# Cross-attention block on Trainium2: Q with its bias row kept in its PSUM bank instead of the SBUF staging tile

## What is computed

```python
g_x     = (g_w @ x_2 + g_b).transpose          # (N, CI)   CI = 256, C = 512, N = 1024
theta_x = (theta_w @ x + theta_b).transpose    # (N, CI)
phi_x   = phi_w @ x_2 + phi_b                  # (CI, N)
W  = theta_x @ phi_x / N
y  = (W @ g_x).transpose
wy = w_w @ y + w_b
wy = bn_gamma * (wy - bn_mean) * rsqrt(bn_var + 1e-5) + bn_beta
out = wy + x
```

## Time and profile before

| what | us |
|---|---|
| median of three runs | 796.55 |
| the profiled execution, its own time | 797.28 |
| its span, first to last instruction | 795.5 |
| PE busy | 778.5 (98%) |
| POOL busy | 540.8 (68%) |
| DVE busy | 524.7 (66%) |
| ACT busy | 305.4 (38%) |

### The profile page before, as it was taken

One profiled execution on the slowest core, in us unless ns is written; L12 is line 12 of the kernel. 1 busy time (PEld: TensorE's weight loads), 2 busy tenths in 40 slices (PEclk: granted clock), 3 DMA queues, 4 the chain that ended last, 5 costly groups with the idle time before them and its releaser, 6 DMA issues.

```text
span 795.5 us, 11592 instructions
## 1 busy us (share of the span) xinstructions
PE 778.5 (98%) x4045; PEld 665.4 (84%) x4045; DVE 524.7 (66%) x889; ACT 305.4 (38%) x514; POOL 540.8 (68%) x358
## 2 busy tenths in 40 slices
PE   4999999999999999999999999999999999999997
PEld 4688888888888888888888888888888888888886
DVE  3787584857758497584857758497584857758254
ACT  3734442325334143442325334143442325334131
POOL 4969785777857579585777857579585777857500
PEclk9999999999999999999999999999999999999999
DMA  9828255171643707255171633707255171630202
GB/s 235 195 107 211 107 117 201 33 219 67 167 150 73 243 0 211 105 115 201 31 220 65 167 149 73 243 0 211 105 117 200 29 223 64 168 150 1 106 1 105
DMA packets 55127, 103.17 MB, mean 130 GB/s; under 512 B 2474, under 2 KB 37956, under 8 KB 55108
## 3 DMA queue, kind: packets, MB, share of 16 engines
q1 hardware_dynamic: 52976, 101.86, 43.7%
q10 hardware_dynamic: 2132, 1.05, 0.8%
HBM read 69.35 MB, written 33.55 MB: 129 GB/s over the span
## 4 chain that ended last, share of the span: by engine, by line
PE 96%; DVE 2%; ACT 1%; DMA 1%; issue 0%; DVEq 0%; SPq 0%; ACTq 0%
PE wbank L667 56%; PE gbank L667 36%; PE wbank L830 1%; DMA ctx_sb<-in_ctx_dram 1%; PE wbank L708 1%; PE wbank L686 0%; ACT ctxT_hi L340 0%; DVE x_sb L486 0%; PE wbank L714 0%; ACT x_sb L366 0%; DVE ctxT L486 0%; DVE th_lo L583 0%; DVE tmp L509 0%; DVE tmp L508 0%; ACT x_hi L340 0%
## 5 line engine op out<-in xcount | busy, mean ns | idle before, releaser
L286 POOL TENSOR_TENSOR ctxT_lo<-ctxT,ctxT_hi 128x512 fp32r<-128x512 f32 x124 | 167.6, 1353 | 200.1 <-ACT ctxT_hi L340 200.1
L297 POOL TENSOR_TENSOR ctx_sum<-ctx_sum,ctxT 128x512 f32<-128x512 f32 x108 | 163.7, 1516 | 0.2
L315 POOL TENSOR_TENSOR x_lo<-x_sb,x_hi 128x1024 fp32r<-128x1024 f32 x60 | 142.4, 2406 | 0.0
L340 ACT ACTIVATE mt<-wbank 128x512 fp32r<-128x512 f32 x64 | 37.9, 597 | 242.7 <-PE wbank L667 242.7
L657 DVE SCALAR_TENSOR_TENSOR x_sb<-wbank,const,x_sb 128x512 f32<-128x512 f32 x112 | 79.2, 747 | 67.6 <-PE wbank L667 67.6
L667 PE MATMUL wbank<-ctxT_lo,ctxT_hi 128*128 128x512 f32 x512 | 121.0, 392 | 0.0
L518 DVE TENSOR_TENSOR stage<-gbank,mt 128x384 f32<-128x384 f32 x64 | 28.3, 485 | 139.8 <-PE gbank L667 139.7
L667 PEld LDWEIGHTS wbank<-ctxT_lo,ctxT_hi 128*128 128x128 f32 x512 | 95.1, 189 | 18.6 <-POOL ctxT_lo L286 0.2
L340 ACT ACTIVATE ctxT_hi<-ctxT 128x512 fp32r<-128x512 f32 x124 | 76.5, 628 | 87.9 <-DVE ctxT L486 87.9
L667 PE MATMUL gbank<-ctxT_hi 128*128 128x384 f32 (+1 forms) x512 | 80.5, 313 | 10.2 <-ACT ctxT_hi L340 10.2
L667 PEld LDWEIGHTS gbank<-ctxT_hi 128*128 128x128 f32 x512 | 79.8, 191 | 12.0 <-issue 10.2
(11 more groups left out here) (107 smaller groups left out, 1363.3 us busy)
## 6 DMA issues: line engine op xcount, KB each, us to landing
x_sb<-in_x_dram SPq DMA_DIRECT2D x16, 2048.0 KB, 7.8
out_dram<-x_sb SPq DMA_DIRECT2D x64, 512.0 KB, 2.6
ctx_sb<-in_ctx_dram SPq DMA_DIRECT2D x60, 512.0 KB, 8.5
ctx_sb<-in_ctx_dram ACTq DMA_DIRECT2D x4, 256.0 KB, 7.4
ctx_sb<-in_ctx_dram SPq DMA_DIRECT2D x4, 256.0 KB, 7.3
x_sb<-in_L_xattn_w_w_dram SPq DMA_DIRECT2D x1, 512.0 KB, 11.8
stage<-in_L_xattn_theta_w_dram SPq DMA_DIRECT2D x1, 512.0 KB, 12.7
phi_nat<-in_L_xattn_phi_w_dram SPq DMA_DIRECT2D x1, 512.0 KB, 12.8
```

The costliest lines, as they stand in the source:

```text
L286: nc.gpsimd.tensor_tensor(ctxT_lo[:, c, :], turned_ctx(b, c), f(ctxT_hi[:, c, :]), ALU.subtract).then_inc(sem_, 1)
L297: nc.gpsimd.tensor_tensor(ctx_sum[:, :], ctx_sum[:, :], src, ALU.add).then_inc(ctxT_used, 1)
L315: nc.gpsimd.tensor_tensor(x_lo[:, k, :], x_sb[par][:, k, :], f(x_hi[:, k, :]), ALU.subtract).then_inc(x_lo_made, 1)
L340: nc.scalar.activation(dst, src, ACT.Copy).then_inc(sem_, 1)
```

## The change

The sum of Q and its bias row is written back into Q's own PSUM bank, in place; ScalarE's copy to q_hi and VectorE's subtraction to q_lo read it from there. T is still staged in SBUF. The number of instructions and their order are the same on each engine, and so are all semaphores; only these operands change, in 32 instructions of each of the three kinds.

```diff
@@ scalar, body
                 for k in range(KI):
                     act.wait_ge(q_taken, KI * b + (k + 1))
-                    hi(q_hi[:, k, :], stage[:, k * C:(k + 1) * C], q_hi_made)
+                    hi(q_hi[:, k, :], gbank[Q_BANK[k]][:, :], q_hi_made)
                 theta(1)
@@ vector, body
                 def q_lo_part(k):
                     dve.wait_ge(q_hi_made, KI * b + (k + 1))
-                    nc.vector.tensor_tensor(q_lo[:, k, :], stage[:, k * C:(k + 1) * C], f(q_hi[:, k, :]),
+                    nc.vector.tensor_tensor(q_lo[:, k, :], gbank[Q_BANK[k]][:, :], f(q_hi[:, k, :]),
                                             ALU.subtract).then_inc(q_lo_made, 1)
 
                 dve.wait_ge(s_taken, b + 1)
                 for k in range(KI):
                     dve.wait_ge(q_done, KI * b + (k + 1))
-                    nc.vector.scalar_tensor_tensor(out=stage[:, k * C:(k + 1) * C], in0=zb_row[:, :],
+                    nc.vector.scalar_tensor_tensor(out=gbank[Q_BANK[k]][:, :], in0=zb_row[:, :],
                                                    scalar=p1[:, k:k + 1], in1=gbank[Q_BANK[k]][:, :],
                                                    op0=ALU.mult, op1=ALU.add).then_inc(q_taken, 1)
```

## The result

| | before | after |
|---|---|---|
| median, us (6 runs each) | 796.08 (795.48 to 796.88) | 789.90 (789.42 to 790.77) |
| span of the profiled execution | 795.5 | 788.3 |

The ratio is 0.9927, with a 95% interval of 0.9917 to 0.9937: 6.2 us faster. The forecast was 790.4, with a range of 789.4 to 792.9.

What follows compares the result with a forecast made beforehand. TensorE, 98% busy, was taken to bound the kernel, losing time only to late q_lo and th_lo. Batches 1 to 14 regain 6.1 us in all: 796.55 - 6.1 = 790.4 us, range 789.4 to 792.9.

Steps and rivals of the forecast that it cites:

- the two places: Each batch's first output products, needing q_lo of k = 0, and their third group, needing th_lo: 0.12 and 0.18 us late.
- Why q_lo was long: VectorE's q_lo reads two SBUF tiles beside GpSimd; its second SBUF operand waits for GpSimd, 692 to 1784 ns.
- The rival in which the lock stays: q_hi or zb_row in SBUF suffices for the VectorE-GpSimd lock, or it isn't q_lo's cause: 796.5 us, chance 0.05.
- q_lo from PSUM at 0.69: VectorE's subtraction with a PSUM operand takes 0.69 us, priced from z_lo's 684 ns and undisturbed q_lo's 692.
- The sum to PSUM at 0.74: VectorE's sum at L646 written to PSUM takes 0.74 us each, as th_lo; bounds 684 and 1784 ns.
- q_hi at 597: ScalarE's copy to q_hi from PSUM takes 597 ns, against 1.29 us for two from SBUF; worth nothing.
- Margins: Slack before the weight loads are late: 0.76 us for q_lo of k = 0, 0.38 us for th_lo's load.
- Nothing late next: With both losses gone no other load becomes late, since batch 15 shows this order with no idle load.
- The sum: Batches 1 to 14 each regain 0.41 to 0.51 us of TensorE's stretch, 6.1 us in all: 790.4 us.
- The rival of a little more: GpSimd's earlier end also frees VectorE's other subtractions from SBUF: 789.6 us, chance 0.04.
- The rival of the sequencer: Only the second loss goes; TensorE's four waits at the first output products keep 2.5 us: 792.9 us, chance 0.08.
- The rival of the slow write: VectorE's sum takes twice its 0.74 us into PSUM, losing 0.63 us in all sixteen batches: 800.5 us, chance 0.03.

Runs made afterwards that it cites:

- GpSimd thin: GpSimd's instructions cut to one column each from batch 1's preparation on: 789.61 us on the kernel before (Q staged in SBUF), 789.80 us on the changed kernel.
- one transpose: Changed kernel plus one needless VectorE transpose of 128x512 between the two sums and q_lo of k = 0: 789.79 us.
- the repeat: The changed kernel timed once more, unaltered, beside its variants on the same chip: 789.79 us, ratio to the kernel before 0.9926.
- two transposes: Changed kernel plus two needless VectorE transposes between the two sums and q_lo of k = 0: 796.13 us, ratio to the kernel before 1.0007.

## Why the prediction was right

- **Where TensorE loses.** Right. It was read from the weight load's idle rows and from batch 15, the batch without GpSimd. The two kernels with one half of Q in PSUM separate the two places as forecast. Only the count was too high: 27 of the 29 idle loads lie there.
- **Why q_lo was long.** Right, and shown: 693 ns from SBUF with GpSimd thin, 692 from PSUM with GpSimd at work. The rival in which the lock stays is refuted by the same numbers.
- **q_lo from PSUM at 0.69.** Measured 692 ns. **The sum to PSUM at 0.74.** Measured 751 ns; both bounds were far, and the value taken, that of the nearest operation, held. That was in part luck, since no row showed a write to PSUM; a sum of up to 1.12 us would have left the forecast as it was. The side estimate of 0.065 us more for each sum didn't show: 7 ns. **q_hi at 597.** Measured 598.
- **Margins.** 0.76 us for q_lo: the delay of one transpose (0.53 us) fits, that of two (1.13 us) doesn't. th_lo's place: its idle time of 1.06 us stands in the rows above.
- **Nothing late next.** Right: every stretch is 8.16 us, and the rest of a batch takes 39.14 us as before (204.86 - 157.15 - 8.57 before, 202.84 - 155.54 - 8.16 after).
- **The sum.** 6.1 us forecast, 6.11 measured in the stretches, 6.18 between the medians. 790.4 against 789.90: the half microsecond is the median of before, 796.55 from three runs and 796.08 from six. That the medians agree to a tenth is luck: they move with how many of the runs have the slower clock at the start, and in the repeat they differ by 5.75 us (795.54 - 789.79). It is the stretches that carry the agreement.
- **The rival of a little more.** At 789.90 the time alone doesn't tell it from the forecast. The traces do: VectorE's other subtractions from SBUF are not faster after (gram_lo 1295 ns before and 1304 after, t_lo 1072 and 1071), and the rest of the batch is unchanged.
- **The rival of the sequencer.** It was wrong as a forecast, but it pointed at something real, told below: the loop's batches have an extra time at this load, and only when the wait is unmet.
- **The rival of the slow write.** Refuted by the 751 ns. Its rule for the price was inexact: I counted 0.2 us of lateness as absorbed, from a load that starts 0.32 late. But q_lo itself was only 0.08 late in batch 7 (it takes 1.53 us and ends at 398.18, due at 398.10), and the load started 0.24 us behind it. With two transposes q_lo of batch 7 is 0.3 late and TensorE loses about 0.3 and then 0.1 of wide matmuls: in the loop the late start of the load eats up what would be absorbed, and lateness of q_lo passes one to one. In batch 1, written out, q_lo is 0.29 late (110.75 + 0.65 against 108.62 + 2.49) and the stretch loses 0.25 in all. At 0.74 us late, as that rival assumed, an estimate from batch 7 gives a loss of some 0.8 us in each batch of the loop, in place of 0.63.

By the Trainium skill (VectorE: DVE Perf Modes, Rules for kernel authors) one works on a matmul's output in PSUM or, if many operations follow, copies it to SBUF first. Three operations on Q follow here, and the runs decide against the copy: 692 ns from PSUM against 1579 in the mean from SBUF, since GpSimd is busy. With GpSimd thin the two are equal, 692 and 693, so in this kernel the staging had nothing to gain even in quiet.

## What to carry to other kernels

An engine that is 98% busy can still lose time to waits that its busy rows don't show: look at the weight load's idle rows, and for a batch in the same trace in which the suspected neighbour is idle. A VectorE instruction with two SBUF operands beside a busy GpSimd can take twice its time and more (1579 ns in the mean against 692); one operand in PSUM frees it, but the bank must be free for longer: where a later block wants it (T here), the longer hold costs more than the lock did. And of several slow instructions only the one with a due time is worth repairing: k = 0 alone brought all of the gain.

## What the runs showed of the hardware that was not expected

At the first output products an unmet wait costs more inside the hardware loop than in the batches that are written out. With two transposes, the load starts at 111.46 in batch 1, which is written out, 0.06 us after q_lo's first half has ended (110.75 + 0.65); in batch 2, the loop's first, it starts at 159.16, 0.21 us after (158.30 + 0.65):

```profile
110.75 1.25 DVE L640 TENSOR_TENSOR q_lo<-gbank,q_hi 128x512 fp32r<-128x512 f32 x2
111.46 0.30 PEld L670 LDWEIGHTS wbank<-th_hi,q_hi 128*128 128x128 f32 x2 [0.38 <-DVE q_lo L640]
```

```profile
158.30 1.25 DVE L640 TENSOR_TENSOR q_lo<-gbank,q_hi 128x512 fp32r<-128x512 f32 x2
159.16 0.30 PEld L670 LDWEIGHTS wbank<-th_hi,q_hi 128*128 128x128 f32 x2 [0.54 <-issue]
```

The releaser is named q_lo in the one and "issue" in the other, for the same cause. Where the wait is met in time, as in the changed kernel, batches of the loop and written-out ones take the same 8.16 us. So "issue" before a load did not mean here that nothing had been waited for.

The extra is not one of the loop as such. In the kernel before, the load that waits for th_lo starts 0.11 us after th_lo's end in batch 1 and in batch 7 alike (115.02 - 114.91 and 401.31 - 401.20), and "issue" is named in both:

```profile
113.51 1.40 DVE L583 SCALAR_TENSOR_TENSOR th_lo<-wbank,vec_cols,th_hi 128x512 fp32r<-128x512 f32 x2
115.02 0.30 PEld L667 LDWEIGHTS wbank<-th_hi,q_hi 128*128 128x128 f32 x2 [0.49 <-issue]
```

```profile
401.31 0.30 PEld L667 LDWEIGHTS wbank<-th_hi,q_hi 128*128 128x128 f32 x2 [0.28 <-issue]
```

With T in PSUM, the load that waits for t_lo starts 0.05 us after it in batch 1 (100.61) and in batch 2 (148.46). At these two places the unmet wait is the last one before the load; at the first output products q_lo's is the first of four, with counts that depend on the loop's turn. That the three waits behind it take the 0.15 us fits all three places, but isn't shown: taking some of them out was not tried.

The lock works both ways. With only k = 0 in PSUM, q_lo of k = 1 came ahead of GpSimd's sum_hi in batch 7, took 0.87 us, and sum_hi took 1.74 us; its mean was 1721 ns in the kernel before, and it is 1296 in the kernel after, with both halves in PSUM:

```profile
L296 POOL TENSOR_TENSOR sum_hi<-ctx_sum,ctxT 128x512 fp32r<-128x512 f32 x15 | 19.4, 1296 | 0.0
```

GpSimd as a whole was busy 540.8 us before and 527.5 after. That it is the reading of SBUF by GpSimd, and not any work of it, that holds VectorE was not tried; all its instructions here read SBUF.
